# Two attention blocks in float32: the output projection in three float32r passes over both tiles, and a new order of the group's work on TensorE

## The reference

```python
x = _attn(_ln(x, g1, b1), _ln(x, g1, b1), Wq1, Wk1, Wv1, Wo1, bo1) + x    # SELF
x = _attn(_ln(x, g2, b2), context, Wq2, Wk2, Wv2, Wo2, bo2) + x          # CROSS
x = _geglu_ff(_ln(x, g3, b3), Wp, bp, Wf, bf) + x                        # GEGLU
```

## Time and profile before

| | |
|---|---|
| median of 3 runs | 482.31 us (480.09 to 482.73) |
| profiled execution, its own time | 484.91 us |
| its span, first to last instruction | 483.2 us |
| granted TensorE clock, mean over the span | 0.989 |
| PE busy | 459.1 us (95%) |
| DVE, ACT, POOL busy | 360.4, 278.2, 193.7 us |
| SELF and CROSS | about 17 to 340 us of the span |

### The profile page before, as it was taken

The page is one execution under the profiler, slowest core; times in us unless marked ns, Lnnn a source line. Parts: engine busy times, 40 slices in busy tenths (PEclk is TensorE's granted clock), DMA queues, the critical chain, the costliest instruction groups (busy, mean ns, idle before and its releaser), DMA issues.

```text
span 483.2 us, 17683 instructions
## 1 busy us (share of the span) xinstructions
PE 459.1 (95%) x7662; PEld 417.5 (86%) x7662; DVE 360.4 (75%) x652; ACT 278.2 (58%) x505; POOL 193.7 (40%) x218
## 2 busy tenths in 40 slices
PE   7699899999999999999999999979999999998897
PEld 7698798988998989999889898868999777777797
DVE  4578677887888888878877778776785678688562
ACT  4365645546547655665475554744455657676773
POOL 4734462324423733546234442333332313132473
PEclk9989999999999999999999999998999999999999
DMA  7850000000000000000000000000000000000011
GB/s 232 194 167 5 2 3 3 1 3 3 3 3 1 11 13 1 11 11 1 13 1 11 11 1 12 2 3 1 2 0 8 18 11 17 2 3 1 1 43 44
DMA packets 17300, 10.57 MB, mean 22 GB/s; under 512 B 7888, under 2 KB 16272, under 8 KB 17232
## 3 DMA queue, kind: packets, MB, share of 16 engines
q1 hardware_dynamic: 16800, 9.48, 7.2%
q10 hardware_dynamic: 432, 0.07, 0.1%
HBM read 8.50 MB, written 1.05 MB: 20 GB/s over the span
## 4 chain that ended last, share of the span: by engine, by line
PE 85%; DVE 7%; issue 4%; ACT 2%; DMA 1%; ACTq 0%; POOL 0%; DVEq 0%
PE out0p L756 13%; PE stage L574 12%; PE stage L575 11%; PE stage L576 11%; PE scp L664 7%; PE scp L706 6%; PE scp L870 6%; PE stage L739 4%; PE scp L739 4%; DVE mx L1146 3%; PE out0p L772 2%; PE scp L680 2%; DMA bias<-in_L_xattn_bo_dram 1%; DVE vb L1123 1%; PE stage L790 1%
## 5 line engine op out<-in xcount | busy, mean ns | idle before, releaser
L1385 POOL TENSOR_TENSOR pr<-pr,rc 128x1024 f32<-128x1024 f32 x32 | 60.3, 1905 | 72.8 <-DVE rc L1171 72.8
L947 ACT ACTIVATE pr<-pr 128x1024 f32<-128x1024 f32 x48 | 50.7, 1055 | 54.0 <-DVE pr L1141 51.3
L756 PE MATMUL out0p<-wo_of,ot 128*128 128x128 f32 x512 | 65.7, 281 | 0.6 <-issue 0.6
L756 PEld LDWEIGHTS out0p<-wo_of,ot 128*128 128x128 f32 x512 | 59.6, 191 | 2.9 <-issue 0.8
L1136 DVE TENSOR_REDUCE mx<-scp 128x16 f32<-128x1024 f32 x32 | 39.2, 1224 | 21.5 <-PE scp L664 21.4
L891 ACT ACTIVATE q_of_heads<-stage 128x512 f32<-128x512 f32 x64 | 35.0, 599 | 35.1 <-PE stage L576 34.7
L891 ACT ACTIVATE vt<-stage 64x512 f32<-64x512 f32 x64 | 37.9, 593 | 29.5 <-PE stage L576 28.0
L664 PE MATMUL scp<-k_of_heads,q_of_heads 64*64 64x64 f32 x2048 | 39.2, 221 | 9.2 <-issue 8.2
L1176 DVE COPY vt<-stage 64x512 f32<-64x512 f32 x64 | 44.4, 694 | 2.6 <-PE stage L576 0.6
L664 PEld LDWEIGHTS scp<-k_of_heads,q_of_heads 64*64 64x64 f32 x2048 | 34.5, 135 | 12.3 <-issue 9.4
L1115 DVE COPY k_of_heads<-stage 128x512 f32<-128x512 f32 x32 | 22.1, 692 | 27.3 <-PE stage L576 27.3
(11 more groups left out here) (238 smaller groups left out, 1313.7 us busy)
## 6 DMA issues: line engine op xcount, KB each, us to landing
ctx_in<-in_ctx_dram SPq DMA_DIRECT2D x16, 96.0 KB, 2.0
wo_of<-in_L_xattn_Wo_dram SPq DMA_DIRECT2D x2, 512.0 KB, 10.1
out_dram<-rows SPq DMA_DIRECT2D x8, 128.0 KB, 1.8
rows<-in_x_dram SPq DMA_DIRECT2D x1, 768.0 KB, 9.7
pr<-in_L_xattn_Wq_dram SPq DMA_DIRECT2D x1, 512.0 KB, 4.7
pr<-in_L_xattn_Wk_dram SPq DMA_DIRECT2D x1, 512.0 KB, 6.3
pt<-in_L_xattn_Wv_dram SPq DMA_DIRECT2D x1, 512.0 KB, 7.8
rows<-in_L_xattn_Wq_dram SPq DMA_DIRECT2D x1, 512.0 KB, 8.4
```

Source lines behind the costliest of these rows:

```text
L756: last = nc.tensor.matmul(out0p[:, t * D:(t + 1) * D], ot[:, a // 2, a % 2, t, :], wo_w[s.phase][:, a, :], start=(a == 0), stop=(a == PAIR ...
L947: nc.scalar.activation(pr[t][:, :], pr[t][:, :], ACT.Exp, scale=scale[s.phase]).then_inc(exped, 1)
L1385: nc.gpsimd.tensor_tensor(halves(pr[t][:, :]), halves(pr[t][:, :]), rc[:, t, :, None].to_broadcast([ROWS, H, N]), ALU.mult).then_inc(probs, 1)
```

## The change

- Wo of SELF and CROSS: Wo is split into a high part and a rest like the other weights. One `out_step(s)` makes the transposed result of both tiles: eight chunks, three float32r matmuls each, Wo as weights and the attention's result (256 columns) as the moving side. ACT copies the 128 x 256 result out of PSUM, `out_turn_step` turns it back with two transposes, and DVE adds it to the rows. The attention's result is kept as a high part (ACT copies it out of PSUM, four banks for a group instead of two) and a rest (DVE subtracts, four for a group, in place of its two copies).
- Order on PE: `scores_step(one, 0)` moves to the end of the group, before `x_step(two)`; `av_step(before, 1)` moves behind `x_step`, to the start of the next group; `proj_step(one)` starts right behind it with piece 0, then `scores_step(s, 1)`, piece 1, `out_step(before)`, pieces 2 to 4, `out_turn_step(before)`, pieces 5 to 7. `av_step(s, 0)` comes before `val_step` 3, and its results go to the round of `stage` banks.
- ACT copies all eight pieces of the projections (DVE had two of them). DVE's order follows. POOL makes the normalised rows of `two` behind the products with the reciprocal, not before them.
- Loads: SP waits for the first group's first exp ahead of Wo1 and everything that follows it. The bias bo1 is no longer among the vectors that the first `x_step` of ACT waits for. Wo lies in tiles that are free at that time; its high part and rest are made in the SELF groups 0 and 7 (one copy on ACT, one subtract on POOL, 128 x 1024).
- Front: all eight pieces of the first projection come before the second `x_step`; the first normalising is DVE's; fewer `keep_warm` matmuls.
- Last group of CROSS: values, second scores and Wo of the group before come in another order, with one `out_step` and one `out_turn_step` at its end.

```diff
@@ PE
-            def out_step(s, t):
+            def out_step(s):
...
-                pe.wait_ge(act, cnt.at("act", s, 2 * t, kind="av"))
-                pe.wait_ge(dve, cnt.at("dve", s, 2 * t + 1, kind="av"))
-                for a in range(PAIRS):
-                    last = nc.tensor.matmul(out0p[:, t * D:(t + 1) * D], ot[:, a // 2, a % 2, t, :],
-                                            wo_w[s.phase][:, a, :], start=(a == 0), stop=(a == PAIRS - 1))
+                if s.first == 0:
+                    pe.wait_ge(rest_o, 1 + s.phase)
+                if s.is_group(CROSS, GROUPS - 1):
+                    keep_warm(out0p, 5)
+                wh, wr = wo_s[s.phase]
+                for i in range(2):
+                    pe.wait_ge(dve, cnt.at("dve", s, 2 + i, kind="av"))
+                    for m in range(PAIRS // 2):
+                        a = 2 * m + i
+                        mh, mr = (o[:, m, i, :, :].rearrange("p t r -> p (t r)") for o in (ot_h, ot_r))
+                        nc.tensor.matmul(out0p[:, 0:GR], wh[:, a, :], mh, start=(i == 0 and m == 0), stop=False)
+                        nc.tensor.matmul(out0p[:, 0:GR], wh[:, a, :], mr, start=False, stop=False)
+                        last = nc.tensor.matmul(out0p[:, 0:GR], wr[:, a, :], mh, start=False,
+                                                stop=(i == 1 and m == PAIRS // 2 - 1))
+                last.then_inc(out_turned, 1)
+            def out_turn_step(s):
+                pe.wait_ge(out_copied, cnt.at("out_copied", s))
+                for t in range(T):
+                    last = nc.tensor.transpose(out0p[:, GR + t * D:GR + (t + 1) * D], outT[:, t * ROWS:(t + 1) * ROWS],
+                                               ident[:, :])
+                last.then_inc(out0, 1)
...
@@ PE group(s)
-                    scores_step(s, 0)
                     if before:
-                        out_step(before, 0)
-                    scores_step(s, 1)
-                    if before:
-                        out_step(before, 1)
+                        av_step(before, 1)
                     if last:
-                        p_step(one, s, (0, 1))
+                        val_step(s, (0,))
+                        scores_step(s, 1)
+                        val_step(s, (1,))
+                        out_step(before)
                     else:
-                        proj_step(one, s)
-                    val_step(s, (0, 1))
-                    turn_step(s, 0)
-                    val_step(s, (2,))
+                        proj_step(one, s, range(1))
+                        scores_step(s, 1)
+                        proj_step(one, s, range(1, 2))
+                        if before:
+                            out_step(before)
+                        proj_step(one, s, range(2, 5))
+                        if before:
+                            out_turn_step(before)
+                        proj_step(one, s, range(5, 8))
+                        val_step(s, (0, 1))
...
                     turn_step(s, 1)
+                    av_step(s, 0)
                     val_step(s, (3,))
-                    av_step(s, 0)
                     if last:
                         p_step(one, s, (2, 3))
+                        av_step(s, 1)
+                    else:
+                        scores_step(one, 0)
                     x_step(two, s)
-                    av_step(s, 1)
                     if last:
-                        out_step(s, 0)
-                        out_step(s, 1)
+                        out_step(s)
+                        out_turn_step(s)
@@ ACT group(s), groups other than the last
-                        exp_step(s, 0)
-                        p_step(one, (0,))
+                        sc.wait_ge(scores, cnt.at("scores", s, 1))
+                        p_step(one, range(2))
+                        if before:
+                            out_step(before)
                         exp_step(s, 1)
-                        p_step(one, range(1, 8))
-                    val_step(s, (0, 1))
-                    pt_step(s, 0)
-                    val_step(s, (2,))
+                        p_step(one, range(2, 8))
...
@@ DVE
-            def av_step(s, t):
-                ve.wait_ge(full, cnt.at("full", s, 2 * t + 1, kind="av"))
-                nc.vector.tensor_copy(*av_copy(s, 2 * t + 1)).then_inc(dve, 1)
+            def av_step(s, t, which=range(2)):
+                for i in which:
+                    ve.wait_ge(act, cnt.at("act", s, 2 * t + i, kind="av"))
+                    of, bank = av_copy(s, 2 * t + i)
+                    nc.vector.tensor_tensor(ot_r[:, :, i, t, :], bank, of.bitcast(F32), ALU.subtract).then_inc(dve, 1)
...
@@ DVE group(s)
                     max_step(s, 0)
                     shift_step(s, 0)
+                    if before:
+                        av_step(before, 1)
...
                     max_step(s, 1)
                     shift_step(s, 1)
...
                     pt_step(s, 1)
+                    av_step(s, 0, (0,))
                     val_step(s, (3,))
-                    av_step(s, 0)
+                    av_step(s, 0, (1,))
...
@@ SP
             load_rows(2 * T, TILES - 2 * T, loaded_rows[2])
+            sp.wait_ge(exped, cnt.at("exp", Step(SELF, 0), 0))
             load_weight(SELF, "o")
```

More of the change, by code:

```diff
@@ L880, in _ @@
             x_step(Step(SELF, 0), None)
-            keep_warm(out0p, WARM_UP)
-            proj_step(Step(SELF, 0), None, range(4))
+            keep_warm(out0p, WARM_UP // 2)
+            proj_step(Step(SELF, 0), None)
             x_step(Step(SELF, 1), None)
-            proj_step(Step(SELF, 0), None, range(4, 8))
+            scores_step(Step(SELF, 0), 0)
             each_group(pe, group)
@@ L1019, in group @@
                         copy(w1_s[0][:, :], w1[:, :]).then_inc(high_w, 1)
-                    av_step(s, 1)
+                    if last:
+                        out_step(s)
                 elif s.phase == CROSS2:
@@ L1273, in _ @@
             stats_step(Step(SELF, 0))
+            norm_step(Step(SELF, 0))
             for c in range(2):
@@ L1378, in group @@
                 three = far(s)
-                if s.phase in (SELF, CROSS) or (s.phase == CROSS2 and two.phase == FFN):
+                if s.phase == CROSS2 and two.phase == FFN:
                     rstd_step(two)
                 if s.phase in (SELF, CROSS):
-                    norm_step(two, one)
                     for t in range(T):
```

210 lines of the change are left out of this document (128 added, 82 removed).

## The result

The changed kernel takes 496.24 us (median of 4 runs, 494.62 to 496.46), the kernel before 482.25 (480.09 to 482.73): a ratio of 1.029, with an interval of 1.026 to 1.032. It is slower, as the larger chance said (0.46, against 0.34 for the same and 0.20 for faster), but by 14 us where 2.5 were forecast, and outside the range. The profiled execution has a span of 494.7 us, 11.5 more than before; those 11.5 are what the two traces can explain. The other 2.5 of the medians' 14.0 lie in the kernel before: its profiled execution (484.91) was 2.7 above its median, that of the changed kernel (496.46) 0.2.

What follows compares the result with a forecast made beforehand. PE's own work plus its waits was taken as the bound. Terms 8.4 + 0.5 - 5.9 - 4.5 - 0.5 = -2.0, with clock +4.5, gave +2.5 on the median 482.31: 484.8 us, range 478.5 to 491.

Steps and rivals of the forecast that it cites:

- the larger chance: Whole kernel: slower, above 484.7 us, chance 0.46; the same had 0.34 and faster 0.20.
- Output product: Wo in each group: 3.96 us becomes 2.88 plus two transposes at 0.30, net -0.78.
- TensorE's own work: PE in each group, waits taken off: 19.05 less 0.78 and 0.24 gives 18.03 us in SELF, 18.25 in CROSS.
- The wait for the rest: PE ahead of projection piece 0: a new wait of 0.82 us in SELF and 2.07 in CROSS.
- Piece 1 and the subtraction: PE ahead of projection piece 1: waits for a DVE subtract, 0.2 us (0 to 0.5) in SELF, none in CROSS.
- The clock: PE after the new CROSS waits: 3 falls to the lower clock (between 0 and 8), 1.5 us each, +4.5.
- Issue gaps: PE's gaps put down to issue in 14 periods: 1.2 of 7.1 us remain, -5.9 (ends -7.1 and 0).
- The front: Start to first `turn_step`: -6.0 us if gap and slow clock go, 1.5 comes back: -4.5 (ends -6.5 and -0.6).
- Last group: Last CROSS group, from its predecessor's `turn_step` to its output's end: 31.95 us becomes 31.4, -0.5 (-2.5 to +1.5).
- first group: Group 1's subtracts, pushed by the weight copies on ACT in SELF 0: +0.5 us.
- The last step: Whole kernel: adds the difference of +2.5 us to the median of the kernel before, 482.31, giving 484.8.
- Rival C: Whole kernel: clock falls in nearly every CROSS group, +12, 492 us; or loads bring gap and slow clock, 489; chance 0.13.

Runs made afterwards that it cites:

- e7: The changed kernel with the second half of the scores cut into three parts, two more runs of small matmuls; 508.76 us, ratio 1.060.
- e6: The changed kernel with values piece 3 put back ahead of P times V of the first tile; 490.62 us, ratio 1.018.
- e1: The changed kernel with `scores_step(s, 1)` ahead of piece 0 of the projection instead of between pieces 0 and 1; 482.69 us, ratio 1.002.
- e15: The changed kernel with one 64-column float32r matmul on a 64*64 tile added ahead of projection pieces 3, 4, 6 and 7; 525.8 us.
- e16: The changed kernel with one 64-column float32r matmul on the whole array added ahead of projection pieces 3, 4, 6 and 7; 502.2 us.
- e9: e10 plus the edits of e2 and e6, on the changed kernel; 486.78 us, ratio 1.010.
- e10: The changed kernel with `scores_step(s, 1)` moved ahead of `av_step(before, 1)`, rest not split; 485.11 us, ratio 1.007.
- e13: e14 with values 3 moved behind first P times V, next scores and transposition, and both subtractions ahead of values 3's copy; 482.76 us, ratio 1.0005.
- e14: The changed kernel with e2's edit and half of the second scores on either side of `av_step(before, 1)`; 479.02 us, ratio 0.993.
- e4: The kernel before with only the deferred loads, and bo1 not among the first `x_step`'s vectors; 482.85 us, ratio 1.001.
- e2: The changed kernel with piece 0 waiting only for the rows' rest and pieces 4 to 7 for the context's; 484.26 us, ratio 1.003.
- e3: The changed kernel with five identity matmuls behind `av_step(before, 1)` in groups that wait for the context's rest; 492.08 us, ratio 1.020.
- e11: The changed kernel with one 64-column float32 matmul on a 64*64 tile added ahead of projection pieces 3, 4, 6 and 7; 523.3 us.

## Why the prediction was wrong, step by step

- **Output product**: by starts, the two `out_step` before took 1.98 + 1.81, the new one and its transposes 2.88 + 0.14, -0.77. The forecast was -0.78, in part by luck: it had the old product at 3.96 for 3.79 and the transposes at 0.30 for 0.14, two errors that cancel.
- **TensorE's own work** is the step that failed: "PE's own work is then 18.03 in SELF and 18.25 in CROSS". It put at nothing, without a reason, what the new neighbours cost the other blocks. By starts in the two timelines of a SELF group, waits off, the turns with values 2 and 3 went from 3.23 to 3.42 us, the scores, P times V and `x_step` from 4.59 to 4.88, the pieces with values 0 and 1 from 7.20 to 7.51: +0.79, all where blocks of different kinds meet. The own work measured 18.82 and 19.06. That such edges do it is shown both ways: one run more costs 0.35 us (e7), one fewer gives 0.35 (e6) or 0.33 (e1, CROSS; in SELF 0.15, with a delay of 0.24 in the scores), and a matmul that has to go to the small tile and back costs 0.25 more than one that has not (e15 less e16). e6 and e1 undo different cuts of the new order, e6 the one behind the transposes and between P times V and the next scores, e1 the one inside the projections; in CROSS they give 0.35 + 0.33 = 0.68 of the 0.81, each measured alone, and that they add is not shown. Counting runs is not enough: e6 has three like the kernel before, and its work beside the output product is still 15.38 us for 15.02. The last 0.1 of the edges was read from starts only. Over 14 groups: +11.2 us.
- **The wait for the rest**: 0.74 against 1.02 in SELF, 2.00 against 2.07 in CROSS. Right, and in the two parts forecast. The 0.24 ahead of the fifth piece did go.
- **Piece 1 and the subtraction**: no wait in the changed kernel beyond its first group (0.2 forecast); 0.3 to 0.8 in e9, e10, e13 and e14, where piece 1 comes sooner.
- **The clock**: three falls behind the CROSS waits, as many as forecast, but the 3 was picked between 0 and 8, so that it came true is luck; the price was right, a period with a fall is 1.46 us longer (22.53 against 21.07). The fourth, behind the wait for GpSimd's products in the last group, was not forecast.
- **Issue gaps**: 0.8 us are left in the periods (1.2 forecast). Of the 7.1 us that the prediction called gaps, the brackets of the 14 periods show 4.6; the rest has no bracket, like the delays in e14 and e9. That runs of small matmuls bring them was right and cuts both ways: e10 and e14 bring the gaps back with the dense runs. The Trainium skill's page "Runtime: NRT & Kernel Launch", section "Instruction fetch mechanics", has the crossing of a 16 KB block of instructions mostly hidden. No run here shows a crossing as such. If the gaps are crossings, the traces agree where float32r work lies between (0.8 us in 14 groups), and not in runs of small matmuls or under the loads (1.98 us in e14, 4.84 in e4).
- **The front**: -5.7 us for -4.5; of what the loads under groups 0 and 1 should give back (1.5), nearly nothing showed.
- **Last group**: 33.3 us for 31.4. The prediction gives no list of its waits there, so which one it had too short is not on record; measured are 0.57, 0.51, 0.62, 0.50 and 0.47 for subtractions and copies, and the 1.75 for the products with a fall of the clock behind it (about 1.5).

The forecast of +2.5 us for the profiled execution becomes, with own work +11.2, last group +1.9, front -1.2, waits -2.2 (six times 0.28, eight times 0.07), issue gaps -0.4 and small terms -0.3 (clock falls 4.4 for 4.5, first group 0.37 for 0.5): +11.5, the measured difference of the spans. The last step, to add it to the median of the kernel before, then lost the 2.4: the gains in gaps and slow clock were read from an execution 2.6 us longer than the median, which I take to hold more of both than the median does. For the clock the executions bear it out: of the 89 of the kernel before beside the experiments, those with a mean clock of 0.999 or 1.000 took 479.5 to 480.8 us and those with 0.989, as in the profiled one, 483.0 to 484.5 (none reached 484.91). For the gaps it is argued, not shown. Rival C came nearest in size (492), by falls in nearly every CROSS group, which did not come.

## What to carry to other kernels

Price a matmul block by the distance between starts, and with its neighbours: a block of 64*64 matmuls moved away from its like, between float32r work, costs TensorE 0.33 to 0.36 us more, three times the pace of float32r matmuls of 256 columns. Putting such blocks together again gives that back only where the denser run is not held up (e10 and e14 kept next to nothing of it). Interleaving is worth it only where it removes a wait or an issue gap longer than that. Take gains that are gaps from an execution near the median. When a moved step takes away a cover, fill or refill the hole at once (of the 14 us lost, e2 won back 12 and e14 17, with the same arithmetic), and look for the wait that takes over: in e9, e10, e13 and e14 the saving ahead of piece 1 ran into VectorE's subtraction.

## What the runs showed of the hardware that was not expected

- A matmul on a 64*64 tile between float32r matmuls on the whole array costs 0.36 us in float32r and 0.445 in float32, of which its own columns are 0.03; on the whole array 0.11 and 0.22.
- Waits of TensorE of the same length and place did not all lower the clock: of the eight groups that wait 2.0 us in two parts, three did in the changed kernel, none in the profiled execution of e7. With 1.3 of the 1.64 us filled, none did in that of e3.
- A wait ahead of a float32r matmul can cost more than the profile's bracket for it: 0.24 us more in e7 (0.17 in the bracket) and in e14 (0.49).
- Under the loads of weights TensorE stood still for "issue" in the first period for 1.98 us (e14), 3.23 (e11), 3.55 (e15) and 4.84 (e4), with the DMA engines moving 247 to 342 GB/s; in e4 ScalarE and VectorE were idle behind it. The changed kernel's own trace has no such gap under the same loads, so that the loads cause it is not shown.
